# Four chained graph layers: the attention's chunk loops written out, residual loads two masks earlier, some exponentials and copies moved

## What is computed

```python
x = layernorm(x + gated_graph_layer(x, adj))      # adj @ x, message, GRU cell
x = layernorm(x + gcn_layer(x, adj))              # D^-1/2 (adj + I) D^-1/2 (x W) + b
x = layernorm(x + transformer_conv(x, adj))       # the attention, below
x = layernorm(x + hyperbolic_layer(x, adj))       # Moebius product, adj @ xt, maps

# transformer_conv, 4 heads of 32:
attn  = einsum('nhc,mhc->hnm', q, k) / sqrt(32)
e     = where(adj == 0, 0, exp(attn - rowmax))
out   = einsum('hnm,mhc->nhc', e / sum(e), v)
beta  = sigmoid([out, x_r, out - x_r] @ Wb)
return beta * x_r + (1 - beta) * out
```

## Time and profile before

| | |
|---|---|
| Median of 3 runs | 1965.56 us (1961.86 to 1967.49) |
| The profiled execution: its own time, its span | 1969.61 us, 1967.9 us |
| Before the attention's first unit | 610.9 us |
| The attention, first transpose to last | 610.9 to 1700.0 us |
| The last layer | from 1700.0 us |
| Instructions executed | 46,099 |
| Busy in the span | PE 93%, DVE 61%, ACT 53%, POOL 49% |

### The profile page before, as it was taken

How to read it: one execution, slowest core, us unless ns; L and a number is a source line. 1 busy time by engine, 2 the same in 40 slices (tenths; PEclk the granted TensorE clock), 3 DMA queues, 4 the chain that set the end, 5 groups by cost and what they waited for, 6 DMA issues and landing times.

```text
span 1967.9 us, 46099 instructions
## 1 busy us (share of the span) xinstructions
PE 1836.2 (93%) x15504; PEld 1224.9 (62%) x15504; DVE 1205.4 (61%) x2222; ACT 1039.9 (53%) x1664; POOL 965.4 (49%) x1069
## 2 busy tenths in 40 slices
PE   6999999999987999989999999999999999979995
PEld 2444444444445788877777777777777777634442
DVE  4677773212137788878887888878878888211111
ACT  0111100000006888888878887888878888403322
POOL 0111111111136556677677677777766876353333
PEclk9999999999998999999999999999999999989998
DMA  9667767899975222222222222122122221668881
GB/s 376 244 222 260 261 219 256 302 366 351 376 245 169 94 75 77 66 65 92 70 82 70 65 88 79 63 84 91 52 83 82 65 93 39 259 234 291 318 311 56
DMA packets 110369, 329.45 MB, mean 167 GB/s; under 512 B 13104, under 2 KB 31280, under 8 KB 85552
## 3 DMA queue, kind: packets, MB, share of 16 engines
q1 hardware_dynamic: 87552, 285.25, 41.1%
q10 hardware_dynamic: 20016, 32.78, 4.6%
q0 software_dynamic: 2560, 8.39, 1.6%
HBM read 299.11 MB, written 27.26 MB: 166 GB/s over the span
## 4 chain that ended last, share of the span: by engine, by line
PE 36%; issue 13%; POOL 10%; DVE 4%; DMA 2%; ACT 1%; POOLq 1%; DVEq 0%; SPq 0%; ACTq 0%
PE bank L552 16%; PE bank L566 10%; PE bank L525 9%; POOL arena L1317 3%; DVE arena L1103 1%; POOL early L1310 1%; DMA arena<-adj 1%; POOL arena L1310 1%; DVE arena L1088 1%; DMA arena<-root_dram 1%; POOL small L1317 1%; PE bank L422 1%; DVE small L912 1%; POOL small L1263 0%; ACT arena L788 0%
## 5 line engine op out<-in xcount | busy, mean ns | idle before, releaser
L552 PE MATMUL bank<-ident,arena 128*128 128x128 f32 x4096 | 551.2, 276 | 29.8 <-ACT arena L788 21.1
L552 PEld LDWEIGHTS bank<-ident,arena 128*128 128x128 f32 x4096 | 481.6, 142 | 117.2 <-ACT arena L788 24.2
L776 ACT ACTIVATE arena<-arena,small 128x2048 f32<-128x2048 f32 x256 | 511.6, 1998 | 0.1
L788 ACT ACTIVATE arena<-bank 128x512 f32<-128x512 f32 x704 | 397.0, 596 | 175.4 <-PE bank L552 173.6
L422 PE MATMUL bank<-arena,stat_s 128*128 128x512 f32 x1016 | 451.3, 601 | 11.8 <-POOL stat_s L1317 4.9
L525 PE MATMUL bank<-k,parts 128*128 128x512 f32 x1024 | 374.4, 448 | 38.6 <-issue 16.3
L422 PEld LDWEIGHTS bank<-arena,stat_s 128*128 128x128 f32 x1016 | 193.5, 193 | 244.3 <-issue 237.1
L1310 POOL TENSOR_SCALAR early<-arena 128x512 bf16<-128x512 f32 x128 | 246.5, 1925 | 93.1 <-DVE small L1088 52.3
L566 PE MATMUL bank<-arena,stat_x 128*32 128x128 f32 x8192 | 279.6, 277 | 0.5 <-issue 0.4
L1103 DVE COPY arena<-bank 128x512 f32<-128x512 f32 x320 | 219.8, 687 | 94.4 <-PE bank L552 93.9
L1310 POOL TENSOR_SCALAR arena<-arena 128x512 bf16<-128x512 f32 x128 | 247.3, 1932 | 48.5 <-DVE small L1088 21.6
(11 more groups left out here) (160 smaller groups left out, 1318.4 us busy)
## 6 DMA issues: line engine op xcount, KB each, us to landing
arena<-adj_cols SPq DMA_DIRECT2D x191, 1024.0 KB, 5.8
arena<-adj SPq DMA_DIRECT2D x256, 256.0 KB, 2.6
k_dram<-arena ACTq DMA_DIRECT2D x32, 256.0 KB, 6.5
q_dram<-arena ACTq DMA_DIRECT2D x32, 256.0 KB, 8.9
k<-k_dram POOLq DMA_DIRECT2D x32, 256.0 KB, 8.2
parts<-q_dram SPq DMA_DIRECT2D x128, 64.0 KB, 2.1
x_dram<-arena ACTq DMA_DIRECT2D x16, 256.0 KB, 3.8
arena<-x_dram ACTq DMA_DIRECT2D x16, 256.0 KB, 5.8
```

What stands on the lines that cost most here:

```text
L552: last = pe.transpose(bank[:, b_, h * P:(h + 1) * P], cols[:, st % SETS, h, u * P:(u + 1) * P], ident[:, :])
L776: act.activation(cols[:, s_, h, :], cols[:, s_, h, :], ACT.Exp, bias=shift[:, t % 2, 1, i:i + 1], scale=-1.0, accum_out=blocksum[:, t % 2, ...
L788: act.activation(turned[k % TURNED], bank[:, TURN_BANKS.bank(("unit", k)), :], ACT.Copy).then_inc(unit_copied_act, 1)
```

## The change

The change has three parts. (1) The loops over chunks 1 to 6 (for SyncE 2 to 7) are written out on all five engines: `c` is a number, so the waits have constants and the register instructions and the jump are gone. (2) The residuals' loads stand behind the loads of mask column 5 instead of 8, and wait for the row chain's `h` of the chunk before instead of its last step `xt`. (3) Six exponentials of a chunk stand at other units: 37 to 38, 57 to 58, 65 to 66, 69 to 71, 89 to 88, 93 to 94. The copies of units 38, 58, 84, 87, 91 and 93 go from ScalarE to VectorE, and those of 37, 57 and 69 from VectorE to ScalarE, in every chunk: VectorE has 43 copies of 128 instead of 40. Where a unit has both, the exponential stands ahead of ScalarE's copy.

```diff
+VECTOR_ALSO = (38, 58, 84, 87, 91, 93)
+VECTOR_NOT = (37, 57, 69)
+EXP_MOVED = {37: 38, 57: 58, 65: 66, 69: 71, 89: 88, 93: 94}
...
-def exp_ahead(c, k, last_chunk):
-
-    i = k // 4 + EXP_LEAD
+def exp_ahead(c, place, last_chunk):
+
+    i = place + EXP_LEAD
...
-BY_VECTOR = [k for k in range(UPC) if k % 16 in VECTOR_PLACES]
-BY_SCALAR = [k for k in range(UPC) if k % 16 not in VECTOR_PLACES]
+BY_VECTOR = [k for k in range(UPC) if (k % 16 in VECTOR_PLACES or k in VECTOR_ALSO) and k not in VECTOR_NOT]
+BY_SCALAR = [k for k in range(UPC) if k not in BY_VECTOR]
+EXP_PLACES = [EXP_MOVED.get(k, k) for k in range(1, UPC, 4)]
...
-                    if m == 8 and not first:
+                    if m == 5 and not first:
                         load_residuals(c - 1)
...
                 if not is_zero(c):
-                    sp.wait_ge(att_pool, AG(c - 1, "xt"))
+                    sp.wait_ge(att_pool, AG(c - 1, "h"))
                     sp.wait_ge(att_x3_out, 16 * c)
...
-            with sp.Fori(2, CHUNKS) as c:
+            for c in range(2, CHUNKS):
                 attention_loads(c, False)
...
-            with pe.Fori(1, CHUNKS - 1) as c:
+            for c in range(1, CHUNKS - 1):
                 attention(c, False, False)
...
-                    ahead = exp_ahead(c, k, last_chunk)
-                    if k % 4 == 1 and ahead:
-                        exponent(*ahead)
+                    if k in EXP_PLACES:
+                        ahead = exp_ahead(c, EXP_PLACES.index(k), last_chunk)
+                        if ahead:
+                            exponent(*ahead)
```

6 lines of the change are left out of this document (3 added, 3 removed).

## The result

| | before | after |
|---|---|---|
| Median of the runs | 1964.87 us (4 runs, 1961.86 to 1967.49) | 1888.41 us (4 runs, 1887.24 to 1889.14) |
| The profiled execution: its own time, its span | 1969.61, 1967.9 us | 1889.14, 1887.3 us |
| Attention's first unit begins | 610.9 us | 602.5 us |
| The attention | 1088.8 us | 1016.6 us |
| The last layer | 268.4 us | 268.3 us |

What follows compares the result with a forecast made beforehand. TensorE was taken as the bound, a chunk's excess being its waits. Terms 22.7 + 16.4 + 10.1 + 6.4 + 6.5 + 1.6 = 63.7 us, so 1965.6 - 63.7 = 1901.9 us; range 1889 to 1924.

Steps and rivals of the forecast that it cites:

- 24 groups at 0.27: Units 36 to 39, 56 to 59, 68 to 71: wait for VectorE's copy shortens by moving it to ScalarE; -6.4 us (0 to 10).
- units 92 to 95: Chunks 1 to 7: copy of unit 93 waits behind table loads, tanh and exponential; moving it to VectorE, -6.5 us (0 to 13.3).
- Nothing before or behind the attention changes: Stretches ahead of and after the attention: claimed to keep their time, so no gain was counted there.
- the baseline's 4.0: Whole kernel: profiled execution, 1969.6 us, lies 4.0 above the median of the runs, so the sum starts from 1965.6.
- The loops (22.7 forecast): Units 124 to 127 and 0 to 3: five jumps' idle time, 17.1, and slow starts behind them, 5.6, go; -22.7 us.
- The first rival: Chunk ends: the jump is not the cause, so the gap and slow start stay; 1924.6 us, chance 0.06.
- the comparison of the units 12 to 15: Undisturbed group, looped chunk 3 against written-out chunk 0: both take 3.88 us, so register instructions were costed at nothing.
- The slower rival, fetched code that stalls: Written-out chunks on all engines: each new code block stalls 3.4 us, 265 us in all; 2167 us, chance 0.02.
- The residuals (16.4): Units 44 to 47, chunks 2 to 7: earlier residual loads remove the wait from the late row chain; -16.4 us.
- about 5 us earlier: GpSimd's row chain: with the earlier loads it starts about 5 us earlier, more than the 2.97 us VectorE waited.
- Units 64 to 67 (10.1): Eight chunks: ScalarE's copy of unit 65 now stands ahead of an exponential of 1.99 us; -10.1 us, at worst half.
- VectorE as the bound: Rival, units 84 to 93: VectorE's added copies and masks make scores late and the clock fall; 1931.7 us, chance 0.07.

Runs made afterwards that it cites:

- the two faster versions: Changed kernel with copies 5 and 101 moved to ScalarE, exponentials 5 and 101 to 7 and 103: 1884.3 us; same with every loop written out: 1883.4 us.

## Which step of the prediction failed, and what was right

The measured 1888.4 us lies 0.6 us below the range, 1889 to 1924, and 13.5 us below the 1901.9 that the sum gave. Each part worked by the mechanism that was forecast; what failed are sizes in the sum. The step with the largest error is Part 3's: "24 groups at 0.27" gave 6.4 us where 9.4 came, and the 0.94 us per chunk that was left to units 92 to 95 gave 6.5 where 9.7 came. Two terms were put at nothing without a reason: units 108 to 111, where 2.1 came, and the stretch ahead of the attention ("Nothing before or behind the attention changes"), where the two profiles differ by 8.3 us, of which the baseline's 4.0 took in about half.

**The loops (22.7 forecast): right.** 17.1 and 6.0 came. The first rival, that the jump is not the cause, is refuted: the gaps stand where there is a jump and nowhere else, with one chunk per turn and with two. The Trainium skill, "Advanced Engine Details and Errata", section "Control Flow Timing", has about 108 ns for a compare-and-branch. Where the branch is not taken the trace has 83 ns, near it; where it goes back over a short body it has 208, twice that; and where it goes back over a whole chunk it has 3749, and going by the row was right. The register instructions, which I cost at nothing, are worth about half a microsecond per looped chunk, which the comparison of the units 12 to 15 could not show. And the five jumps are not TensorE's alone: the pauses of the other engines at theirs were not in the prediction.

**The slower rival, fetched code that stalls: it did not happen.** No group of straight code is longer by a gap like a jump's, and the code fetched fell instead of rising. The argument that a loop of this size fetches its body anew each turn held: a body kept from turn to turn would have made the loop the one that fetches less.

**The residuals (16.4): right in kind, and only by the first profile right in size.** It rests on one execution; the second would have given 45.8 - 23.3 = 22.5. The agreement of 16.4 with 16.4 says that the whole wait went, as forecast, and no more: both are read from the same profile. My expectation for the row chain was right by a hair. The changed kernel in the timelines of SyncE, GpSimd and VectorE, chunk 3:

```profile
983.34 0.37 SPq L367 DMA_DIRECT2D arena<-x_dram  x1
...
1001.42 1.28 POOL L1322 TENSOR_TENSOR arena<-arena,wbo 128x512 f32<-128x512 f32 x1
...
1026.01 1.29 POOL L1322 TENSOR_TENSOR arena<-arena 128x512 f32<-128x512 f32 x1
...
1027.22 0.69 DVE L1108 COPY arena<-bank 128x512 f32<-128x512 f32 x1
1027.82 0.86 DVE L917 BATCH_NORM_STATS2 small<-arena 128x6 f32<-128x128 f32 x4
```

The loads go out 2.7 us ahead of the chunk's first unit (985.99), and GpSimd does not wait for them. The chain begins 15.4 us after that unit, not 19.5 as before, and `y` is done at 1027.30, half a microsecond before VectorE turns to it. The sentence "about 5 us earlier" was 4.1; the lead I took for comfortable is 0.5 us, and the two faster versions use it up.

**Units 64 to 67 (10.1): right,** 10.0.

**Units 36, 56 and 68 (6.4): the term was too small,** 9.4 came. I had taken 0.27 per group. In two of the three groups the whole wait went: 4.10 us is work alone, the 3.88 of a plain group and two more transposes. In units 56 to 59 I had left 0.3 for VectorE's `x3`; the group takes 4.48 us, all of it busy, so that wait went as well. About 1 us of the 9.4 belongs to the loops: written out alone they bring 1.0 in these groups, and putting the moves back costs 8.3. The upper bound of 10 was the better guess.

**Units 92 to 95 (6.5): the wrong wait was named, and the term was too small.** 9.7 came. I had left 0.94 us per chunk, because unit 94's copy stands behind the exponential. The window shows 4.44, of which 0.39 is idle. ScalarE and then TensorE in the changed kernel, chunk 3:

```profile
1076.66 1.28 ACT L830 ACT_TABLE_LOAD   x1
1078.73 0.21 ACT L830 ACTIVATE small<-small 128x4 f32<-128x4 f32 x1 [0.79 <-POOL small L1322]
1078.95 1.28 ACT L831 ACT_TABLE_LOAD   x1
1080.25 2.00 ACT L780 ACTIVATE arena<-arena,small 128x2048 f32<-128x2048 f32 x1
```

```profile
1082.40 1.14 PE L556 MATMUL bank<-ident,arena 128*128 128x128 f32 x8 [0.39 <-ACT arena L780]
```

TensorE waits for the exponential itself (L780), whose result unit 96 turns, and for no copy. The two table loads and the tanh still stand ahead of it, 3.6 us from 1076.66 to 1080.25, with 0.79 of waiting for GpSimd within. In the last chunk the group takes 3.88 and loses nothing.

**VectorE as the bound: it did not happen.** Its seven copies and the masks fit; no score waited for a mask at units 84 to 94. Units 92 to 95 take 30.8 us in seven chunks, where this rival left the 40.5 and added to it.

**Units 108 to 111 (0): overlooked, 2.1 us.** One of VectorE's operations just ahead took three times as long in the kernel before, chunk 3, while GpSimd ran one beside it:

```profile
1132.12 1.04 POOL L1317 TENSOR_TENSOR arena<-hbias,small 128x512 f32<-128x512 f32 x1
1132.25 1.16 DVE L1132 TENSOR_TENSOR arena<-arena 128x128 f32<-128x128 f32 x1
```

After, in the same place of chunk 3:

```profile
1094.00 0.39 DVE L1137 TENSOR_TENSOR arena<-arena 128x128 f32<-128x128 f32 x1
```

In the kernel before VectorE came late to the copy of a turned unit behind it, without idle time, and TensorE waited 0.16 us for that copy; in the changed kernel VectorE stands idle for 0.70 us ahead of the same copy. The timing of the two engines has shifted against each other, and these two operations no longer meet. The group goes to 31.2 with the loops alone, where they still meet in part (0.61 to 0.92 us), and to 31.1 with the moves alone. What I ought to have asked is what a group of 4.2 us waits for where no part of the change was near.

**The baseline (4.0): the step that hid most.** I set the profiled execution 4.0 above the median and kept "nothing before or behind the attention changes". 8.3 us came ahead of it, for the first profile was a bad one there. In the GCN layer TensorE waited 4.0 us for VectorE (L1055) at 445.0 us and 0.9 us once more, against 0.9 us in all in the second profile, and its mean clock from 400 to 470 us was 0.95 instead of 1.00.

**The sum.** Terms that were too small: 3.0 (units 36, 56, 68), 3.2 (92), 2.1 (108), 0.4 (the rest) and, against it, 0.2 lost elsewhere; 4.3 of the baseline. These give 12.8 of the 13.5 by which the forecast was too high; the other 0.7 is by how much the changed kernel's profiled execution lay above its median. The low end of the range, 1889, was made from "all idle time of these places gone", and that is nearly what happened; it held no room for a place not looked at, nor for the scatter of the profile from which all the terms were read. Redone with the bounds stated there (10.7, 10 and 13.3 in place of 10.1, 6.4 and 6.5) the low end is 1890.9, so the range as worked out missed by 2.5 us. The errors of the attention's own terms, 8.5 us, would by themselves have given 1893.4, inside the range; only with the scatter of the two profiled executions does the time fall outside it.

**Not seen at all: that the terms depend on each other.** I added them up as if each wait stood by itself. The gains in us, each against the runs of the kernel before beside it, and the terms of the prediction added up:

| | measured | terms |
|---|---|---|
| loops alone | 30.6 | 22.7 |
| residuals alone | 15.0 | 16.4 |
| moves alone | 12.5 | 24.6 |
| loops and residuals | 41.1 | 39.1 |
| loops and moves | 39.1 | 47.3 |
| residuals and moves | 41.3 | 41.0 |
| all three | 76.5 | 63.7 |

Putting one part back costs 35.2, 35.4 or 34.7 us, where the terms are 16.4 (residuals), 22.7 (loops) and 24.6 (moves). That residuals and moves together come out at their terms is luck: in that kernel units 124 to 127 and 0 to 3 take 9.1 us more than in the earlier trace rows, units 36, 56, 68, 92 and 108 gain some 5 us beyond their terms, and the rest lies outside the attention, in the profile of before against the median.

What remains open: what a far jump waits for, in its 3.6 to 5.1 us, and what the other engines wait for behind theirs; and how much the loops alone give, beyond a range: the medians say 30.6 us, the attention's share of it in the profiles is 22 to 24, and that kernel's profiled execution (1938.8) lay 4.3 above its own median.

## What to carry to other kernels

Lay equal pieces of a regular stream beside each other, and ask of each piece that is longer what ends its wait, in places that the change does not touch too; then profile the baseline a second time before you size anything on it, since here one wait measured 16.4 and 22.5 us in two executions. A hardware loop is cheap when its body is short (0.21 us a turn here) and dear when its body is long. Long was 3,575 instructions on TensorE, but only 343 to 487 on GpSimd, ScalarE and VectorE, which paused 2.4 to 2.8 us at each jump of the kernel before; so count the body on each engine. Writing it out cost nothing here, since the code was fetched each turn anyway. Waits of one chain that is late against a fixed pace grow when all else gets faster, so a part's worth is best measured both alone and by putting it back: here 12 to 31 us alone and 35 put back.

## What the runs showed of the hardware

- A taken jump back over 3,575 instructions of TensorE lasts 3.6 to 5.1 us, one over a body of 213 to 348 instructions 0.21 to 0.24, one not taken 0.08. It does not grow with the body from one chunk to two.
- The other engines' branches are recorded with 45 to 63 ns, and their pause stands behind the record. In the kernel before it is 2.4 to 2.8 us on ScalarE (body of 398 instructions), 2.7 to 2.8 on VectorE (487) and 2.5 to 2.6 on GpSimd (343), and 0.2 to 0.3 us on SyncE (192). All their bodies of up to 91 instructions in the other layers are behind the jump again within 0.3 us.
- The queues for instructions moved 2.35 MB in straight code and 3.03 in the loop. The Trainium skill, "Advanced Engine Details and Errata", section "ISA Cache", has cache lines of 16 KB and two of them, and sizes of 32 KB, or 128 KB on TensorE. q8's packets, 1.85 MB in 113, are 16.4 KB, which agrees; and TensorE's chunk of 3371 matrix instructions, at 66 bytes each by estimate 222 KB, is larger than either. With the short loops written out too, the queues moved 2.57 MB, more than the 2.35: those bodies had not been fetched anew at each turn.
- After waits of 3.25 and 4.49 us TensorE's next matmuls ran at the lower clock (granted 0.50; eight transposes in 1.91 us instead of 1.04). What that adds varies: units 0 to 3 take 6.27 us instead of 4.08 behind a jump of 5.00, and 4.26 to 6.31 behind the five gaps of 3.2 to 3.4 us in the kernel before. Once the lower clock followed a wait of 1.73 us (units 96 to 99 of chunk 6, 5.57 us).
- VectorE's operation on two SBUF tiles at unit 107 takes 0.39 us alone and 1.14 to 1.19 in chunks 1 to 5 of the kernel before, where a GpSimd operation of 1.04 us began 0.10 to 0.15 us ahead of it. With the loops alone that one began 0.4 to 0.7 us ahead, and VectorE's took 0.61 to 0.92. In all of these it ends about 0.25 us behind GpSimd's. The Trainium skill, "SBUF — State Buffer", section "SBUF: two separate sides", says that these two engines share a port pair, held by one of them for the whole instruction; a VectorE operation with two SBUF inputs takes part where GpSimd's reads SBUF. These rows agree. Others do not: in chunks 1 to 6 of the changed kernel the same operation takes 0.39 us though it lies wholly within a mask operation of GpSimd (L1315, 1.92 us), which reads SBUF too. Spans on GpSimd are rough, and no run tried either pair alone.
